# Dense attention weights on TensorE in place of an index search and a gather

## The reference, cut to what matters

```python
p = pts / norm(pts, axis=points)                 # per channel, over the points of a batch
dist = |p_n|^2 - 2 p_n . p_m + |p_m|^2
nn_idx = top_k(-dist, 16)                        # the 16 nearest points of each point
nbr = pts[nn_idx]                                # 16 x 32 features for each point
logits = leaky_relu([pts @ W_emb + b, nbr @ W_emb + b] @ W_att + b_att, slope 0.1)
attn = softmax(logits, over the 16)
agg = sum(nbr * attn, over the 16)
y = [pts, agg] @ W_conv + b_conv                 # 64 -> 32 channels
out = x1 + relu(batchnorm(y)) + pts              # pts: normalised x1
```

## Time and profile before

| what | us |
|---|---|
| median of 3 runs | 16922.12 |
| lowest and highest | 16915.71, 16925.1 |
| span of the profiled execution | 16903.3 |
| PE busy in it | 10910.8 |
| DVE busy | 12293.0 |
| ACT busy | 3787.2 |
| POOL busy | 11120.9 |

### The profile page before, as it was taken

The page is one execution under the profiler, slowest core; times in us unless marked ns, Lnnn a source line. Parts: engine busy times, 40 slices in busy tenths (PEclk is TensorE's granted clock), DMA queues, the critical chain, the costliest instruction groups (busy, mean ns, idle before and its releaser), DMA issues. The chain is left out here.

```text
span 16903.3 us, 162135 instructions
## 1 busy us (share of the span) xinstructions
PE 10910.8 (65%) x23194; PEld 5109.1 (30%) x23194; DVE 12293.0 (73%) x29441; ACT 3787.2 (22%) x10526; POOL 11120.9 (66%) x11809
## 2 busy tenths in 40 slices
PE   4998466666666666666666666666666666666663
PEld 4887322222222222222222222222222222222221
DVE  1111587778878777777877778788878887787786
ACT  1222322222222222222222222222222222222221
POOL 0000077777777777777777777777777777777775
PEclk9998655555555555555555555555555555555555
DMA  7444611111111111111111111111111111111113
GB/s 127 107 109 115 200 18 18 18 20 17 21 15 23 15 22 16 20 18 19 19 18 20 17 21 15 23 15 22 16 20 18 19 19 17 21 17 21 15 17 103
DMA packets 659735, 587.45 MB, mean 35 GB/s; under 512 B 389675, under 2 KB 603707, under 8 KB 649090
## 3 DMA queue, kind: packets, MB, share of 16 engines
q0 software_dynamic: 380928, 256.85, 11.6%
q1 hardware_dynamic: 277026, 315.18, 7.7%
q10 hardware_dynamic: 1536, 12.85, 0.4%
HBM read 479.08 MB, written 104.90 MB: 35 GB/s over the span
## 5 line engine op out<-in xcount | busy, mean ns | idle before, releaser
L727 POOL DMA_INDIRECT near<-table,row x11760 | 11100.0, 944 | 3631.3 <-issue 3443.1
L774 PE MATMUL psum<-points,queries 34*128 34x512 f32 (+3 forms) x11200 | 8555.1, 968 | 164.2 <-issue 131.1
L774 PEld LDWEIGHTS psum<-points,queries 34*128 34x128 f32 (+1 forms) x11200 | 3501.3, 325 | 5507.2 <-issue 5507.2
L1007 DVE MAX8 found<-scores 128x8 f32<-128x224 f32 x10976 | 3966.3, 383 | 592.5 <-DVE place L1079 537.0
L748 PE MATMUL psum<-doubt,ones 128*1 128x1 f32 x3136 | 186.9, 163 | 4552.1 <-DVE doubt L1064 4552.0
L1065 DVE FIND_INDEX8 place<-best,scores 128x8 uint32<-128x3136 f32 x784 | 2679.5, 3418 | 0.0
L1079 DVE FIND_INDEX8 place<-best,scores 128x8 uint32<-128x3136 f32 x771 | 2635.8, 3419 | 0.0
L853 ACT ACTIVATE scores<-psum 128x512 f32<-128x512 f32 (+1 forms) x5488 | 2454.4, 553 | 101.1 <-PE psum L774 89.9
L824 ACT ACTIVATE expd<-logit 128x16 f32<-128x16 f32 x784 | 169.1, 216 | 9042.1 <-DVE logit L973 9042.1
L946 DVE SCALAR_TENSOR_TENSOR row<-placed,batch_row,swap 128x16 uint32<-128x16 f32 x784 | 183.6, 234 | 2075.0 <-DMA near<-table,row 2073.9
L748 PEld LDWEIGHTS psum<-doubt,ones 128*1 128x1 f32 x3136 | 128.4, 81 | 4700.3 <-issue 4700.2
(11 more groups left out here) (122 smaller groups left out, 4509.8 us busy)
## 6 DMA issues: line engine op xcount, KB each, us to landing
near<-table,row POOLq DMA_INDIRECT x11760
w_in<-in_L_conv_weight_dram SPq DMA_DIRECT2D x784, 144.0 KB, 2.7
windows<-xg SPq DMA_DIRECT2D x42, 928.0 KB, 10.4
table<-table_sb SPq DMA_DIRECT2D x32, 416.5 KB
own<-table SPq DMA_DIRECT2D x112, 119.0 KB
xg<-padded SPq DMA_DIRECT2D x32, 406.0 KB, 17.3
x_in<-in_x_dram POOLq DMA_DIRECT2D x8, 1568.0 KB, 12.7
conv<-conv_sb SPq DMA_DIRECT2D x4, 3136.0 KB, 40.2
```

The lines of the kernel that those rows point to most:

```text
L727: pool.indirect_dma_start(near[:, par, j, :], None, table[:, :], bass.IndirectOffsetOnAxis(ap=row[:, par, j:j + 1], axis=0)).then_inc(near ...
L774: last = nc.tensor.matmul(ps[r0:r0 + rows, at:at + width], queries[:, par, r0:r0 + rows], points[:, b * N + at:b * N + at + width], start= ...
L1007: n = step(nc.vector.max(found[:, c, :], s[:, c * PART:(c + 1) * PART]))
```

## The change

`attend` is rewritten; `prepare` changes a little. Tiles now stay inside a batch: 25 for each batch, the last of them shifted back to end with the batch (its first points are done twice), 800 in all. All loops run over steps; in step s each engine does its part of tiles s+1 to s-7. The loop over pairs of batches is written out, 50 steps long. What a step does:

- PE multiplies 128 queries with all points as before, in eight pieces of 392 columns, 33 rows deep. Queries and points lie twice in SBUF, at partitions 0 and 64, and the pieces take the copies in turn. ACT copies four pieces at a time.
- ACT makes the steep part of all 128 x 3136 logits (`logits`), POOL adds the flat part (`add_slope`), DVE finds the 16th largest score as before but no places, ACT makes from it a bar that is 0 for the 16 and above 1e12 for the others (`bar`), DVE subtracts it and takes the maximum (`mask`), ACT takes the exponential of all 3136 and their sum (`exponentiate`).
- PE turns the 128 x 3136 weights, in 25 pieces of 128, four to a PSUM bank, two banks in turn (`turn`). ACT copies groups 0 to 3 to SBUF, DVE groups 4 to 6. Then PE multiplies them with the 25 pieces of the batch's features, 32 columns of weights each, piece j into the partitions of quarter j mod 4 (`aggregate`). The sum over quarters is left to `y_agg`, which holds the output weights four times.
- Each group of turned weights is made once its exponentials are there (group 0) or the copy of the group two before is done (group 2 and on). Before the sums, one more matmul adds up the totals of the exponentials.
- Every fourth step (and at the end of a batch) PE makes up to 512 columns of y, DVE copies them, SP stores them.

In `prepare` the matmul that makes `half_sq` has a second one beside it, which makes `share`, the flat part of the logits. Each batch's points, shares (to all 128 partitions) and table rows are loaded by eight DMAs from ACT's queue.

The core of the diff, shortened:

```diff
-TILES = PER * N // P            # 98 for a group of four batches
+TILES = -(-N // P)              # 25 for a batch
+ALL = BATCH * TILES
...
 # prepare, PE
-                        nc.tensor.matmul(half_ps[0:PER, c % 4, 0:CH], halves[:], squares[...], start=True, stop=True)
+                        nc.tensor.matmul(half_ps[0:2 * PER, c % 4, 0:CH], halves[:], squares[...], start=True, stop=False)
+                        nc.tensor.matmul(half_ps[0:2 * PER, c % 4, 0:CH], shares[:], feat_sb[...], start=False, stop=True)
...
 # attend, POOL
-                    for j in range(1, NEIGHBOURS):
-                        pool.indirect_dma_start(near[:, par, j, :], None, table[:, :], ...)
+            def add_slope(t):
+                pool.wait_ge(rises_ready, t.count(1, 1))
+                for k in range(2):
+                    m = masked[:, t.ring, part]
+                    nc.gpsimd.tensor_tensor(m, m, shares[:, t.half, part], ALU.add).then_inc(logits_ready, 1)
...
 # attend, PE
+            def score(t, quad):
...
+                gate(pe, scores_in, t.count(2, quad), pe_passed)
+                for u in range(4):
+                    n, r = quad * 4 + u, F1 * (u % RT)
+                    last = nc.tensor.matmul(ps[:, u * BANK:u * BANK + SCH], queries[r:r + KD, t.par, :],
+                                            points[r:r + KD, t.half, score_columns(n)], start=True, stop=True)
+            def turn(t, g):
...
+                for u in range(min(GROUP, TILES - g * GROUP)):
+                    last = nc.tensor.transpose(ps[0:width, ...], masked[:, t.ring, j * P:j * P + width], ident[:])
+            def aggregate(t):
...
+                gate(pe, turned_act, ...); gate(pe, turned_dve, ...)     # all groups of t copied
+                for j in range(TILES):
+                    width, q = min(P, N - j * P), C * (j % PER)
+                    last = nc.tensor.matmul(ps[q:q + C, SUM_BANK:SUM_BANK + P], rows[0:width, t.half, j, 0:C],
+                                            turned_sb[0:width, t.par, j, :], start=j < PER, stop=j + PER >= TILES)
+            def body(tile):                                  # tile(n): tile s - n
+                add_doubts(tile(1))
+                if tile(Y_LAG).ends_group(): convolve_1x1(tile(Y_LAG))
+                past, coming = tile(3), tile(-1)
+                turn(past, 0)
+                score(coming, 0)
+                for g in range(1, ACT_GROUPS): turn(past, g)          # 1, 2, 3
+                score(coming, 1)
+                for g in range(ACT_GROUPS, T_GROUPS): turn(past, g)   # 4, 5, 6
+                aggregate(past)
...
 # attend, ACT
+            def body(tile):
+                here, past, coming = tile(0), tile(3), tile(-1)
+                copy_turned(past, 0, tile(5))
+                exponentiate(tile(2))
+                copy_turned(past, 1, None)
+                bar(tile(1), tile(2))
+                copy_turned(past, 2, None)
+                copy_scores(coming, 0, tile(1))
+                copy_turned(past, 3, None)
+                logits(here, tile(RING))
+                copy_scores(coming, 1, None)
+                if here.c == 6: next_batch(here)
...
 # attend, DVE
+            def body(tile):
+                here, before, past = tile(0), tile(1), tile(3)
+                search(here, 0)                  # MAX8 over 7 of 14 parts
+                copy_y(...)                      # when due
+                settle_doubts(before)            # reads a number of PE's, branches, lets bar(before) go
+                search(here, 1)
+                mask(before)                     # 128 x 3136, two inputs, after bar(before)
+                max(best[0:8]); negate_top(before)
+                copy_turned(past, ACT_GROUPS)    # group 4
+                match_replace; inverted = invert_total(tile(4)); max(best[8:16])
+                copy_turned(past, ACT_GROUPS + 1)
+                bound_low; normalise(inverted, tile(4)); bound
+                copy_turned(past, ACT_GROUPS + 2)
+                above = sum of weights of found >= bound      # then doubt_ready, for add_doubts
```

More of the change, by code:

```diff
@@ L495, in _ @@
                     pool.dma_start(x_sb[:, par, :], x_rows[bass.ds(g * P, P), :]).then_inc(loaded[par], 16)
-TILES = PER * N // P
[L499 to L556, removed]
@@ new lines, in each_step, with fixed, attend @@
+def each_step(engine, body):
+    def fixed(s):
+        body(lambda lag: Tile(0, s - lag) if 0 <= s - lag < ALL else None)
+    for s in range(-1, STORE_LAG):
+        fixed(s)
+    with engine.Fori(0, BATCH // 2 - 1) as i:
+        for k in range(PAIR):
+            body(lambda lag: Tile(i, STORE_LAG + k - lag))
+    for s in range(STORE_LAG + ALL - PAIR, ALL + STORE_LAG):
+        fixed(s)
+def attend(nc, feat, unit, half_sq, share, table, W_emb, b_emb, W_att, b_att, W_conv, b_conv, y):
+    BANK = 512
+    RT = 2
+    SCH = 392
+    QUAD = 4 * SCH
+    F1 = 64
+    KD = C + 1
@@ new lines, in body @@
+            def body(tile):
+                if tile(1):
+                    add_doubts(tile(1))
+                if tile(Y_LAG) and tile(Y_LAG).ends_group():
+                    convolve_1x1(tile(Y_LAG))
+                past, coming = tile(3), tile(-1)
+                if past:
+                    turn(past, 0)
+                if coming:
+                    score(coming, 0)
+                if past:
+                    for g in range(1, ACT_GROUPS):
+                        turn(past, g)
+                if coming:
+                    score(coming, 1)
+                if past:
+                    for g in range(ACT_GROUPS, T_GROUPS):
+                        turn(past, g)
+                    aggregate(past)
@@ new lines, in next_batch, with logits @@
+            def next_batch(t):
+                act.wait_ge(scored, t.batch(4 * TILES, SCORED_FREE))
+                act.wait_ge(logits_ready, t.batch(2 * TILES, LOGITS_FREE))
+                act.wait_ge(summed, t.batch(4 * TILES, SUMMED_FREE))
+                load_batch(t.batch(1, 1), 1 - t.half)
+            def logits(t, used):
+                if used is not None:
+                    act.wait_ge(turned, used.count(T_GROUPS, T_GROUPS))
+                at = t.c if t.c < TILES - 1 else OWN
+                nc.scalar.activation(masked[:, t.ring, :], shares[:, t.half, :], ACT.Relu, bias=own[:, t.half, at:at + 1],
+                                     scale=STEEP / SLOPE).then_inc(rises_ready, 1)
@@ new lines, in search, with settle_doubts @@
+            def search(t, quad):
+                gate(dve, scores_in, t.count(2, quad + 1), dve_passed)
+                for c in range(quad * EARLY, (quad + 1) * EARLY):
+                    n = step(nc.vector.max(found[:, t.par, c, :], scores[:, t.par, c * PART:(c + 1) * PART]))
+                return n
+            def settle_doubts(t):
+                dve.wait_ge(doubts_made, t.count(1, 1))
+                nc.vector.tensor_scalar(doubts[:], ps[0:1, FLAG:FLAG + 1], float(P * NEIGHBOURS), None, ALU.subtract).then_inc(doubts_in, 1)
+                gate(dve, doubts_in, t.count(1, 1), dve_passed)
+                in_doubt = dve.value_load(doubts[0:1, 0:1], min_val=0, max_val=1 << 20)
+                s, n = scores[:, t.par, :], steps[0]
+                dve.wait_ge(chain, n)
@@ L1081, in body @@
+                steps[0] += 5
                 dve.wait_ge(chain, steps[0])
[L1082 to L1091 removed]
```

754 lines of the change are left out of this document (366 added, 388 removed).

## The result

The changed kernel takes 22,075.8 us (median of 4 runs, 22,060.7 to 22,088.5), the kernel before 16,919.4 us beside it. The ratio is 1.305, with a 95% interval of 1.303 to 1.307. The prediction said 19,650 us, slower by 16%: the side holds, the size was 2,426 us short, and the range (16,000 to 22,200) holds with 124 us to spare.

What follows compares the result with a forecast made beforehand. POOL's gathers bound the old kernel at 18.73 us a tile; the new one was to be bound by engines waiting in turn. 800 steps of 21.7 us, 17,360, plus 2,290 gave 19,650 us, range 16,000 to 22,200.

Steps and rivals of the forecast that it cites:

- What bounds before, and what goes: In attend, POOL's gathers set 18.73 us a tile; they go, and two POOL additions of 3.4 to 7.2 us come.
- nothing on the path: POOL's two additions in attend, 3.4 to 7.2 us together, were claimed to add no time to a step.
- The ring: In attend, PE, ACT and DVE wait for each other in fixed orders, so their pieces add: 22.35 us at 1.2 GHz.
- The rival without a ring: Lags let attend's engines slide and ACT bounds with 14 us a step: 13,500 us in all; chance 0.05.
- PE's and ACT's pieces: Attend step: sums 4.0, doubts and group 0 1.3, ACT 8.8 plus 0.4 for group 1, second scores and group 4 4.1 us.
- DVE's piece: DVE's operations in an attend step, from copy of group 4 to copy of group 6: 2.9 us, reciprocal 0.28.
- The clock: PE's clock in attend stays low through idle gaps; a rise late in the sums and group 0 takes off 0.65 us.
- The sum: Whole kernel: 800 steps of 21.7 us make 17,360, plus 2,290 us outside them: 19,650 us, slower by 16%.
- the rest: Time outside attend's steps: 2,219 us, plus 20 for prepare's second matmul and 50 for the slow way for doubts.
- the likeliest case: Attend steps of 20.4 us (18,600 in all) to 24.5 us (21,950 in all); chance 0.66.
- the rival with the high clock: PE's clock stays high in attend, its pieces halve: 17.3 us a step, 16,150 us, faster by 4.6%; chance 0.24.
- My own test: Signs in attend's trace that would refute the prediction: ACT never idle, clock 1.00, or POOL's additions ending DVE's waits.

Runs made afterwards that it cites:

- experiment 1: The changed kernel with POOL's two additions also waiting for DVE's last operation of the step: 19,493 us, 1.153 times the kernel before.
- experiment 3: The changed kernel with PE making a tile's sums one step later, ahead of the second half of the scores: 20,656 us.
- experiment 4: The changed kernel with ACT's exponential ahead of copy 0 and PE turning group 1 directly behind group 0: 19,593 us.
- Experiment 7: The kernel of experiment 1 with 24 matmuls a tile that nobody reads, placed in PE's two idle gaps: 16,668 us.
- experiment 2: The changed kernel with POOL's additions as early, but in eight pieces of 392 columns in place of two of 1568: 20,145 us.

## Why the prediction was right in sign and short in size

- **What bounds before, and what goes:** the gathers went, and POOL is 25% busy. Two additions cost 7.0 us, the upper end (7.2) of what the earlier trace rows gave. "nothing waits for them until the next step: nothing on the path" was the step that failed: they hold up DVE's bound, on the path, by 3.1 us in each step. No data wait was overlooked; DVE waits for POOL without needing its result.
- **The ring:** right. Experiments 1, 3 and 4 each shorten one link and no engine's work, and the step follows by 1.8 to 3.3 us, with no engine over 72% busy in attend (DVE in experiments 3 and 4, its waiting counted as busy). The rival without a ring (13,500) is out.
- **PE's and ACT's pieces:** sums and the way to them 3.43 us (4.0 predicted, midway between two and four abreast; 3.35 for the sums is nearer to the 2.7 of four than to the 5.4 of two); doubts and group 0 1.27 (1.3); ACT with the wait for group 1 9.22 (9.2); second half of scores and group 4 4.20 (4.1). These four were right within 0.6 us, and the two prices without a row (columns, rows abreast) are now measured.
- **DVE's piece, the mis-sized term:** 6.32 us for 2.9. The bound has 3.32 for 0.16 and the reciprocal 0.95 for 0.28; the others together come to 0.4 less than priced. By my estimate from the Trainium skill ("VectorE: DVE Perf Modes", walkthrough of the pipeline, the repeat count of eight) the reciprocal would have cost about 0.9 us more; the measured 0.67 more lies nearer to that than to nothing.
- **The clock:** I took 0.65 us off each step for a rise towards the end of the burst. In the step shown, and in the two behind it, nothing rose: the clock is 0.50 throughout. In the fourth, where y columns follow the sums without a gap, it is 0.71, and behind them group 0 takes 0.66 us for 1.11 and the first half of the scores 1.59 for 2.98. So the rise came only in steps with y columns, and the stretch has 0.57. The Trainium skill's rule ("TensorE: Matmul & The Clock Gate", Part 4) on transposes stays open, since no run has them alone. The y columns, with what the clock gives back there, and the changes of batch cost 0.46 us a step (mean less median) for 0.85.
- **The sum:** +3.42 for DVE, -0.48 for the other pieces (21.5 to 24.44 without y), +0.65 and -0.39: 24.9 for 21.7. 3.2 x 800 = 2,560 us, less 123 us in the rest (2,167 for 2,290): the 2,437 us between 19,650 and the span 22,087.
- **How much of it was luck:** the range held by 124 us, and not for the reasons it was built on. 24.90 us lies above the likeliest case, whose upper end (24.5) has the sums two abreast and a slow reciprocal; a wait that the prediction put at nothing filled their place. Without this wait the kernel takes 19,493 us (experiment 1), near the 19,650 forecast, so the other misses, 0.67 for the reciprocal and 0.65 for the clock against about 1.3 in shorter pieces, nearly cancel. Two of the prediction's sums are slightly off: the pieces of the rival with the high clock add up to 17.2 us, not 17.3, and the upper end to 24.65 (22,010 us), not 24.5. Neither moves the forecast.
- **The rival with the high clock:** it put 17.3 us a step. Experiment 7 shows that the state exists (18.12 us at 0.97, without the wait for POOL) and that filling PE's gaps reaches it. Left alone, the change does not reach it.
- **My own test** said the prediction is wrong "if POOL's additions end the waits of DVE". They did, but not in a column of waits, where I would have looked; the wait stands as a duration.

The Trainium skill states the cause of the long bound ("SBUF — State Buffer", the two separate sides): the port pair that DVE and GpSimd share is an exclusive lock, held for a whole instruction, and a DVE operation with two SBUF inputs needs it beside a GpSimd instruction that reads SBUF. I had not weighed it. Experiments 1 and 2 agree: 3.32, 0.84 and 0.21 us as the addition under way is long, short or elsewhere, while MAX8 and the normalisation from PSUM go on beside POOL.

## What to carry to other kernels

When engines hand one tile to each other in fixed orders, add up the ring before the engines: the step was 24.9 us with no engine over 64% busy. On such a path a DVE operation with two SBUF inputs and two columns can cost nearly as much as the POOL instruction beside it (3.32 of 3.5 us); place POOL's work beside reductions and PSUM copies, and look for operations whose duration does not fit their size. And where PE waits in each step, fill the gap before rejecting a TensorE design: from 22,076 us one wait, one reordering and idle matmuls led to 14,639.

## What the hardware showed that I had not expected

- A DVE operation of 128x2 with two SBUF inputs takes 0.21 us alone, 3.32 us if an addition of POOL over 1568 columns has just begun. In pieces of 392 columns POOL takes 1.02 us each, not a quarter of 3.5 (0.87). The shortest of the 6,400 pieces takes 1.00 us and the median 1.02, though only some of the eight in a step have a two-input DVE operation beside them: so it is a cost of each instruction. An estimate from the two sizes is 2.1 ns a column and 0.19 us an instruction.
- A reciprocal of 128 columns takes 0.95 us, a product of the same shape 0.28.
- Matmuls whose result is never read held the granted clock at 0.97 and made a kernel with 45% more matmul records 14% shorter (19,469 to 16,666 us).
- The kernel that gathers by 15 indirect DMAs a tile took 16,900 us on some chips and 20,400 to 20,550 on others; those without gathers did not show such a difference in any duration I compared.
